# Attention with lagged keys: the query norm as a row in the masked gates, and squares summed by feature with an adding DMA

## What is computed

```python
q, k, v = _silu(x @ Wq), _silu(x @ Wk), _silu(x @ Wv)       # each then through a causal convolution of 4 taps
z, a, b = x @ Wz, x @ Wa, x @ Wb
q = q * cos + rot_half(q) * sin                              # the same for k
q = q / jnp.maximum(jnp.linalg.norm(q, axis=-1, keepdims=True), 1e-12)   # the same for k
for s in range(K):
    attn = jnp.einsum('bshd,bshd->bsh', q, _lag(k, s)) * scale
    gate = jax.nn.sigmoid(_lag(a, s) * b)
    out = out + (attn * gate)[..., None] * _lag(v, s)
rms = jax.lax.rsqrt(jnp.mean(out * out, axis=-1, keepdims=True) + EPS_NORM)   # over all heads
out = out * rms * norm_w * _silu(z)
return out @ Wout
```

## Time and profile before

| | |
|---|---|
| median of 3 runs | 2850.12 us (2850.07 to 2850.35) |
| span of the profiled execution | 2847.8 us |
| granted TensorE clock, mean | 0.999 |
| attention loop of the second layer | from about 755 to 1850 us |
| TensorE busy | 2826.6 us, 99% |
| VectorE busy | 2252.7 us, 79% |
| ScalarE busy | 1528.7 us, 54% |
| GpSimd busy | 1443.2 us, 51% |

### The profile page before, as it was taken

How to read it: one execution, slowest core, us unless ns; L and a number is a source line. 1 busy time by engine, 2 the same in 40 slices (tenths; PEclk the granted TensorE clock), 3 DMA queues, 4 the chain that set the end, 5 groups by cost and what they waited for, 6 DMA issues and landing times. The chain is left out here.

```text
span 2847.8 us, 40066 instructions
## 1 busy us (share of the span) xinstructions
PE 2826.6 (99%) x13466; PEld 2348.4 (82%) x13466; DVE 2252.7 (79%) x3265; ACT 1528.7 (54%) x3149; POOL 1443.2 (51%) x1016
## 2 busy tenths in 40 slices
PE   9999999999999999999999999999999999999998
PEld 7888888888788888888888888778778887888887
DVE  7899587777888889888988898977667677666665
ACT  6656333333666666666666666765545445444443
POOL 7787233334344444444444444666545556555554
PEclk9999999999999999999999999999999999999999
DMA  3000000000322222222222221321111111211111
GB/s 138 1 23 25 12 19 27 30 27 23 125 65 68 70 64 64 65 73 64 64 64 72 77 71 53 93 75 52 52 45 52 60 45 56 86 45 60 52 52 45
DMA packets 79099, 160.44 MB, mean 56 GB/s; under 512 B 11313, under 2 KB 19889, under 8 KB 77873
## 3 DMA queue, kind: packets, MB, share of 16 engines
q1 hardware_dynamic: 78896, 157.88, 18.5%
HBM read 115.63 MB, written 8.65 MB: 44 GB/s over the span
## 5 line engine op out<-in xcount | busy, mean ns | idle before, releaser
L1546 DVE SCALAR_TENSOR_TENSOR x_tok<-OP,expert_weight,x_tok 128x512 f32<-128x512 f32 x252 | 188.1, 748 | 138.2 <-PE OP L47 138.1
L1425 POOL TENSOR_TENSOR middle_w_lo<-second_raw,middle_w_hi 128x512 fp32r<-128x512 f32 (+1 forms) x96 | 143.4, 1496 | 208.7 <-ACT middle_w_hi L1420 208.7
L1518 POOL TENSOR_TENSOR middle_in_lo<-middle_slot,middle_in_hi 128x512 fp32r<-128x512 f32 x128 | 168.6, 1318 | 131.7 <-ACT middle_in_hi L1514 130.9
L3017 POOL TENSOR_TENSOR lag_rnorm<-lag_norm,minus_half 128x8 f32<-128x8 f32 x64 | 105.1, 1643 | 209.5 <-DVE lag_norm L3408 209.5
L45 PE MATMUL B<-xT_hi,lag_w_hi 128*128 128x512 f32 x516 | 201.4, 390 | 1.8 <-DVE xT_lo L496 1.5
L47 PE MATMUL B<-xT_hi,lag_w_lo 128*128 128x512 f32 x516 | 201.6, 391 | 0.0
L45 PE MATMUL A<-xT_hi,lag_w_hi 128*128 128x512 f32 x512 | 200.6, 392 | 0.4 <-DVE xT_lo L496 0.4
L46 PE MATMUL B<-xT_lo,lag_w_hi 128*128 128x512 f32 x516 | 200.8, 389 | 0.0
L47 PE MATMUL A<-xT_hi,lag_w_lo 128*128 128x512 f32 x512 | 199.9, 390 | 0.0
L46 PE MATMUL A<-xT_lo,lag_w_hi 128*128 128x512 f32 x512 | 199.4, 389 | 0.0
L45 PE MATMUL OP<-middle_down_hi,middle_in_hi 128*128 128x512 f32 x496 | 193.6, 390 | 1.9 <-POOL middle_down_lo L1445 1.7
(11 more groups left out here) (670 smaller groups left out, 9103.8 us busy)
## 6 DMA issues: line engine op xcount, KB each, us to landing
lag_raw<-in_head_weights SPq DMA_DIRECT2D x64, 256.0 KB, 4.5
lag_b_row<-lag_b_scratch SPq DMA_DIRECT2D x64, 256.0 KB, 3.3
lag_rot_q<-lag_r SPq DMA_DIRECT2D x128, 128.0 KB, 2.3
lag_rot_k<-lag_r SPq DMA_DIRECT2D x128, 128.0 KB, 2.4
middle_down_raw<-in_expert_down SPq DMA_DIRECT2D x32, 512.0 KB, 3.4
middle_raw<-in_expert_in SPq DMA_DIRECT2D x32, 384.0 KB, 3.0
second_raw<-in_expert_in SPq DMA_DIRECT2D x32, 384.0 KB, 3.0
double_raw<-in_dense_in SPq DMA_DIRECT2D x12, 512.0 KB, 3.4
```

Source lines behind the costliest of these rows:

```text
L1425: pool.tensor_tensor(self.w_lo[q % 2][:, out], self.raw[q % 2][:, of], f32(self.w_hi[q % 2][:, out]), ALU.subtract).then_inc(self.s_wlo, 1)
L1518: pool.tensor_tensor(self.inner_lo[q % 3][t], self.slot((1, 3)[t], q), f32(self.inner_hi[q % 3][t]), ALU.subtract).then_inc(self.s_lo, 1)
L1546: dve.scalar_tensor_tensor(row, self.down_bank(v, n), self.expert_weight[:, e:e + 1], row, op0=ALU.mult, op1=ALU.add).then_inc(self.s_acc, 1)
L3017: pool.tensor_tensor(rnorm[f.rbuf], norm2, half[:, 0:2 * TPB], ALU.pow).then_inc(s_rn, 1)
```

## The change

The factor of q goes into the masked gates. SP stores it (`store_query`) as a row of 4 x 131 numbers to HBM and loads it back to all partitions (`load_query`). GpSimd multiplies the row with the band (`band_of_query`). `gains` takes the scores instead of the mask, and `probabilities` takes the masked row instead of the scores, so O is already normed by the query. `accumulate` then needs no factor.

The squares are then summed by feature: ScalarE writes the square of O into `square1`, and GpSimd issues a DMA that adds it to `square_sums` in HBM, one 128x512 array for each batch (`add_squares`). At the end of the loop each sum is loaded (`load_sums`), turned once (`turn_sums`) and reduced (`sum_features`). So `turn_mixed` and `sum_squares` go, except for the last step, 63, which is still done as before (its row isn't loaded, its copy of O is turned). On VectorE `gains` moves from between two `accumulate` to behind the first tap of `c2`, and `probabilities` to behind `cross1`; the taps of `cv` follow. Some semaphores are merged.

```diff
+                def store_query(st):
+                    sp.wait_ge(s_rn, st.s + 1)
...
+                    sp.dma_start(window[:, 0:P].rearrange("t p -> p t"), of_query, allow_slow_non_contiguous=True).then_inc(s_query, 16)
+                    sp.dma_start(window[0:TPB - 1, P:BAND].rearrange("t p -> p t"),
+                                 of_query[0:PAD, 1:TPB], allow_slow_non_contiguous=True).then_inc(s_query, 16)
+
+                def load_query(st):
+                    sp.wait_ge(s_query, st.s * 48 + 32)
+                    until(sp, s_prob, 2 * st.s)
+                    sp.dma_start(lag["query"], query_norm[st.s % 2:st.s % 2 + 1, :, :].rearrange("a t n -> a (t n)")
+                                 .to_broadcast([P, TPB * BAND])).then_inc(s_query, 16)
...
                     factor_row(f)
+                    if l1:
...
+                        store_query(l1)
+                        load_query(l1)
+                    if f.s in SUMMED:
+                        load_sums(SUMMED[f.s])
...
                         projection(l1, 3, B, s_z)
-                        if f.s < SWITCH:
-                            if l2:
-                                turn_mixed(l2)
-                            mix(l1)
...
+                        if f.s >= END - 1:
+                            out_projection(l2, (2, 3))
+                        mix(l1)
...
                 def mixture(st):
                     act.wait_ge(s_o, st.s + 1)
-                    until(act, s_ot, st.s)
-                    act.activation(mixed, O, ACT.Copy).then_inc(s_mix, 1)
+                    act.wait_ge(s_pair, min(st.s + 2, STEPS))
+                    if st.s == END:
+                        act.wait_ge(s_squares, END * 16)
+                    act.activation(squares[1], O, ACT.Copy if st.s == END else ACT.Square).then_inc(s_mix, 1)
...
+                def band_of_query(st):
+                    pool.wait_ge(s_query, st.s * 48 + 48)
+                    pool.tensor_tensor(query[:, :, :], query[:, :, :], band_t.unsqueeze(1).to_broadcast([P, TPB, BAND]),
+                                       ALU.mult).then_inc(s_band, 1)
+
+                def add_squares(st):
+                    pool.wait_ge(s_mix, st.s + 1)
+                    until(pool, s_squares, st.s * 16)
+                    sums = square_sums[st.b * P:(st.b + 1) * P, :]
+                    if st.head:
+                        pool.dma_start(sums, squares[1], accum_op=ALU.add).then_inc(s_squares, 16)
+                    else:
+                        pool.dma_start(sums, squares[1]).then_inc(s_squares, 16)
...
+                    elif st.s < END:
+                        until(dve, s_acc, st.s * TPB + t - 1)
+                        dve.tensor_tensor(row, OP[t % 2], row, ALU.add).then_inc(s_acc, 1)
...
                 def gains(st):
                     dve.wait_ge(s_gate, st.s + 1)
-                    dve.scalar_tensor_tensor(gate[:, :, :], gate[:, :, :], 1.0,
-                                             band_t.unsqueeze(1).to_broadcast([P, TPB, BAND]),
-                                             op0=ALU.add, op1=ALU.mult).then_inc(s_gain, 1)
+                    dve.wait_ge(s_s, st.s + 1)
+                    dve.scalar_tensor_tensor(gate[:, :, :], gate[:, :, :], 1.0, scores[:, :, 0:BAND],
+                                             op0=ALU.add, op1=ALU.mult).then_inc(s_prob, 1)
...
+                    if st.s < END:
+                        dve.wait_ge(s_band, st.s + 1)
+                        dve.tensor_tensor(prob[:, :, :], gate[:, :, :], query[:, :, :], ALU.mult).then_inc(s_prob, 1)
```

More of the change, by code:

```diff
@@ L1788, in __init__, with layers @@
         self.wbuf, self.ybuf, self.rbuf = self.head % 2, s % 2, s % 4
-def layers(nc, mem, a, lag_b, saved, store):
+def layers(nc, mem, a, lag_b, saved, query_norm, square_sums, store):
     x_tok, ident = mem["x_tok"], mem["ident"]
@@ L1977, in layers @@
         s_o, s_mix, s_ot, s_osq = sem("o"), sem("mix"), sem("ot"), sem("osq")
+        s_query, s_band = sem("query"), sem("band")
+        s_squares, s_rows = sem("squares"), sem("rows")
         s_y, s_yhi, s_ylo = sem("y"), sem("yhi"), sem("ylo")
@@ L2068, in _ @@
                 save(1)
+                sp.wait_ge(s_init, 2)
+                for n in range(2):
+                    sp.dma_start(query_norm[n, TPB - 1:TPB, P:BAND], rot_q[0:1, SEQ:]).then_inc(s_rows, 16)
                 factors.store(sp, 0)
@@ L2355, in _ @@
                 mix(last_step)
+                turn_sums(2, STEPS)
                 rows.turn(pe, 0, [A, B, S0, S1], norm_2, lambda t: pe.wait_ge(s_sz, STEPS) if t else None)
                 pe.wait_ge(s_mix, STEPS)
-                turn_tiles(T, mixed, s_ot)
+                pe.wait_ge(s_mean, 7)
+                turn_tiles(T, squares[1], s_ot)
                 out_projection(before_last, (2, 3))
@@ L3327, in _ @@
                 for f, l1, l2, l3 in slots():
-                    inside = l1 and f.s < SWITCH
                     if l3 and f.s < END:
                         accumulate(l3, 2)
-                    if l1:
-                        gains(l1)
                     if l3 and f.s < END:
@@ L3338, in _ @@
                     tap(0, f, A, c1, 3, s_c1)
-                    if l1 and not inside:
-                        probabilities(l1)
                     dve.wait_ge(s_tap, f.s * 3 + 2)
                     tap(1, f, B, c2, 1, s_c2)
-                    if inside:
-                        probabilities(l1)
-                    else:
-                        if l2:
-                            accumulate(l2, 0)
-                        tap(1, f, B, c2, 2, s_c2)
+                    if l1:
+                        gains(l1)
                     if f.s == 0:
@@ L3356, in _ @@
                     dve.wait_ge(s_c1, f.s * TAPS + TAPS)
-                    until(dve, s_r2, f.s)
+                    until(dve, s_rotated, 4 * f.s)
                     if f.s == 0:
                         dve.wait_ge(s_rotation, 32)
-                    dve.tensor_tensor(cross2, c1, sin, ALU.mult).then_inc(s_cross, 1)
-                    if inside:
-                        tap(1, f, B, c2, 2, s_c2)
+                    dve.tensor_tensor(cross2, c1, sin, ALU.mult).then_inc(s_rotated, 1)
+                    tap(1, f, B, c2, 2, s_c2)
                     tap(1, f, B, c2, 3, s_c2)
-                    if inside and l2:
+                    if l2:
                         accumulate(l2, 0)
-                    if l2:
                         accumulate(l2, 1)
@@ L3373, in _ @@
                         turn1.low(dve, 2)
-                    if f.s == END - 1:
-                        mean_squares(0)
-                    if not inside:
-                        dve.wait_ge(s_tap, f.s * 3 + 3)
-                        tap(2, f, A, cv, 1, s_cv)
-                    dve.wait_ge(s_c2, f.s * TAPS + TAPS)
-                    until(dve, s_r1, f.s)
-                    dve.tensor_tensor(cross1, c2, sin, ALU.mult).then_inc(s_cross, 1)
-                    if inside:
-                        dve.wait_ge(s_tap, f.s * 3 + 3)
-                        tap(2, f, A, cv, 1, s_cv)
+                    dve.wait_ge(s_c2, f.s * TAPS + TAPS)
+                    until(dve, s_rotated, 4 * f.s - 1)
+                    dve.tensor_tensor(cross1, c2, sin, ALU.mult).then_inc(s_rotated, 1)
+                    if l1:
+                        probabilities(l1)
+                    if f.s == END - 2:
+                        sum_features(3)
+                    elif f.s > END - 2:
+                        mean_squares(f.s - (END - 1))
+                    dve.wait_ge(s_tap, f.s * 3 + 3)
+                    tap(2, f, A, cv, 1, s_cv)
                     tap(2, f, A, cv, 2, s_cv)
@@ L3578, in program @@
             mem[name] = ctx.enter_context(nc.sbuf_tensor(name, shape, F32))
-        layers(nc, mem, a, lag_b, saved, out)
+        layers(nc, mem, a, lag_b, saved, query_norm, square_sums, out)
 def kernel(**inputs):
```

159 lines of the change are left out of this document (84 added, 75 removed).

## The result

| | median, us | lowest to highest | runs |
|---|---|---|---|
| before | 2850.23 | 2850.07 to 2850.41 | 4 |
| changed | 3263.93 | 3258.55 to 3269.32 | 4 |

The ratio is 1.1451, 95% interval 1.1437 to 1.1466: 14.5% slower, 414 us, where 24 us less was forecast. The profiled execution of the changed kernel spans 3258.9 us.

What follows compares the result with a forecast made beforehand. TensorE, busy 2826.6 of 2847.8 us, was taken as the bound. From 2850.1 us, 25.7 for removed turns came off and 1.5 for the end was added: 2825.9 us, range 2821 to 2870.

Steps and rivals of the forecast that it cites:

- The bound and the turns: Attention slots: TensorE sets the time; 59 removed groups of `mixed` turns save 0.435 us each, 25.7 us, slot 16.83 to 16.39.
- the adding DMA's price on GpSimd: Issue on GpSimd between `pair` and the power: 1.0 us (0.3 to 2.5), hidden by 2.7 us of cover.
- The two stores at 2.4 us: SP's stores of the query norm to HBM, after the power: both landed in 2.4 us, ends 2.0 and 4.5.
- The load at 3.3: Load of the norm row to all partitions: 3.3 us, bounds 3.0 to 6.3, so the row is there at +9.1.
- The form of the rivals: Three alternatives on when the row arrives within a slot: late 2903 us, mildly late 2845, early 2855; chances 0.20, 0.18, 0.10.
- Rival A: Row at +9.8 or later, `probabilities` loses port to `pair`, mix waits 1.3 us each slot: 2903 us; chance 0.20.
- The shared port: VectorE and GpSimd instructions with two SBUF inputs exclude each other; the band multiply and `probabilities` were to pass without collision.
- rivals B: Row at +9.3 to +9.8, or VectorE wins the port: 0.1 to 0.5 us lost per slot, middle 2845; chance 0.18.
- rival C: Row before +8.4: band multiply delays `cross2`, 0.5 us lost per slot, 2850 to 2870, middle 2855; chance 0.10.
- a 0.52: Chance given to the main forecast, that the change works without late row, early row or port collisions.
- The end: Behind slot 63: TensorE waits for the last adding DMA and a 256 KB load, 1.5 us (0 to 4).
- VectorE's extra instruction, `accumulate`, the going of `gains`: VectorE's slot: new `probabilities` adds 0.6 us, hidden by 0.9 slack; unscaled `accumulate` and moved `gains` give nothing.

## Why the prediction was wrong

- **The bound and the turns** held. TensorE set the slot in every version where nothing was late, and without the row the slot fell to 16.44, forecast 16.39. Of 0.44 us for each group 0.36 came; 0.06 of what is missing goes with the adding. I had looked for the adding DMA's price on GpSimd (1.0 taken, 0.92 measured), not in the transfers beside it.
- **The two stores at 2.4 us** are the step that failed. The large one took 8.8 us, and 4.5, named as the slow end, was no end. The step rested on the closing stores and on `lag_b_scratch`: whole rows of 2 KB in size, not words. The range left open what a form without a row could cost, and I chose the value of the nearest shape that the trace had, though the form differed in just what mattered. The page "DMA: Bandwidth & Descriptors" of the Trainium skill (Specifications) says that below 512 B an engine reads, modifies and writes; the direction agrees, but words 64 bytes apart are below 512 B too and took 3.2 us, so that rule alone doesn't give the price.
- **The load at 3.3** took 4.8 with the changed kernel's stores, inside the bounds of 3.0 to 6.3, and 3.3 once the store was in pieces.
- **The form of the rivals** failed as well. All of them priced lateness inside one slot and let the next slot start on time. But a late `prob` delays the reductions behind it on VectorE, and so the next row: a ring, whose length is the slot as soon as it is longer than TensorE's work. The prediction's own numbers could have made the sum: 7.5 us from `probabilities` at +12.3 to the power's end at +3.4 of the next slot, 1.3 for the band, and the slow ends 4.5 and 6.3 are 19.6, so 59 times 3.2 us and some 3015; with the 10.1 measured in place of 8.8, some 3090. Rival A said 2903. A range that takes in the bounds of its unknown costs had to reach there.
- **The shared port** was seen rightly and taken too lightly. With a large store of 2.9 us and a load of 3.3, close to what I assumed, the kernel gives 2858, not 2826. The row is there at +9.8 (median; 9.3 to 11.7) where +9.1 was forecast, which is the border of rivals B and A: `cross1` takes 1.11 and `prob` 0.96 us at the mean, and `pair` 1.54. With the norms stored twice the row is there at +7.4, early as in rival C, and it is `cross2` that meets the multiply; the slot then is 0.62 us longer than without the row, C said 0.5. "With little room on each side" was not enough for a 0.52: in a real sequence of slots the load's landing varies by 2 us (3.0 to 5.0), and any of three instructions may meet the multiply.
- **The end**: 1.5 us taken. Without the row the slots give 21 us and the total only 13, so the first and last steps cost some 8, of which the waits for scores are 4.8: there is less of TensorE's work to hide the late moves.
- **VectorE's extra instruction, `accumulate`, the going of `gains`**: as forecast; in the kernel without the row TensorE waits 0.4 us in the whole loop for a tap, and no more for VectorE.

## What to carry to other kernels

Before a transfer goes into a chain, price its form, not its size: a store of 512 single words side by side in DRAM took 8.8 us where the whole tile in 32-byte pieces took 2.9. When an added wait feeds, through the order of an engine, the work that will be waited for in the next round, add up the whole ring; that sum is a lower bound of the period, and it has to be made with the slow ends of every unknown. And if a result is needed only at the end, let it leave the loop in the cheapest form that nobody waits for: one matmul of ones and a 2 KB store did more than the turns' full removal with a row in the chain.

## What the hardware showed that I had not expected

- The time of a store of single words to DRAM goes with their spacing: 8.5 us at 4 bytes, 5.7 at 8, 3.7 at 16, 3.2 at 32 and 64, and 3.0 into SBUF; 128 neighbours cost as much as 512. The packets have all but all started by 2.6 us in each form: a trace of packets doesn't show this time, only the landing does.
- An adding DMA of 256 KB lands after 5.0 us (4.2 to 5.0 by kernel, medians), a plain one from the same queue after 2.5, and beside the adding one the moves take up to 4.7 instead of 3.0.
- In the changed kernel TensorE's granted clock is low around each of the 60 waits for `prob`, which are 2.6 to 6.7 us long. The page shows eight tenths through the loop: 0.50 from 1114.5 to 1119.8 us, behind a wait of 4.5 us, and 1.00 from 1119.8 to 1131. After 4.83 us of idle time the mix takes twice its time of before (1.06), as at the lower of its two levels, 1.2 instead of 2.4 GHz:

```profile
1133.30 0.39 PE L47 MATMUL B<-xT_hi,lag_w_lo 128*128 128x512 f32 x1
1138.52 2.10 PE L2208 MATMUL O<-lag_prob,lag_values 128*128 128x131 f32 x8 [4.83 <-DVE lag_prob L3156]
```

In the slots of the changed kernel it costs nothing, since the ring's branch by TensorE is the shorter one by 1.0 us even at this clock.
